# Gate and up stage of a quantised feed-forward: tokens of block n+2 quantised at the front of VectorE's block n, and GpSimd multiplying tiles 1, 3 and 5 instead of 2 and 4

## The reference, cut to what matters

```
def _act_fake_quant(x, clip_factor):
    scale = jax.nn.sigmoid(clip_factor) * jnp.max(jnp.abs(x)) / QMAX
    return jnp.clip(_ste_round(x / scale), -QMAX - 1.0, QMAX) * scale

xq = _act_fake_quant(x, clip_x[0])
gate = jnp.einsum('bsh,ih->bsi', xq, _weight_fake_quant(w_gate))
up = jnp.einsum('bsh,ih->bsi', xq, _weight_fake_quant(w_up))
h = _act_fake_quant(jax.nn.silu(gate) * up, clip_down[0])
return jnp.einsum('bsi,hi->bsh', h, _weight_fake_quant(w_down))
```

## Time and profile before

| what | us |
|---|---|
| median of 3 runs | 1045.89 (1040.85 to 1046.31) |
| the profiled execution, whole | 1039.43 |
| its span, first to last instruction | 1037.5 |
| start of the gate and up stage (first L1087) | 907.02 |
| its last GpSimd product ends | 982.90 |
| its last VectorE reduction (L1159) ends | 985.73 |
| `partition_all_reduce` starts | 988.85 |

### The profile page before, as it was taken

The page is one execution under the profiler, slowest core; times in us unless marked ns, Lnnn a source line. Parts: engine busy times, 40 slices in busy tenths (PEclk is TensorE's granted clock), DMA queues, the critical chain, the costliest instruction groups (busy, mean ns, idle before and its releaser), DMA issues. The chain is left out here.

```text
span 1037.5 us, 21991 instructions
## 1 busy us (share of the span) xinstructions
PE 797.6 (77%) x8184; PEld 443.3 (43%) x8184; DVE 903.3 (87%) x1428; ACT 644.2 (62%) x981; POOL 518.6 (50%) x330
## 2 busy tenths in 40 slices
PE   2789874777777679998888988988889869167656
PEld 1455541111111245555555555555556548022223
DVE  6679844999999889999989999999999987868968
ACT  3354563999999766555655655655656512467674
POOL 4132330000000019988888998888889877022300
PEclk9898896999999899999999999999999989689979
DMA  9489896564555565585555855577455446000013
GB/s 280 162 280 343 265 346 225 190 213 164 180 217 214 193 178 144 144 269 169 148 163 181 274 139 168 154 215 226 137 171 157 135 164 203 0 1 1 0 41 122
DMA packets 112400, 180.98 MB, mean 174 GB/s; under 512 B 10032, under 2 KB 37296, under 8 KB 112304
## 3 DMA queue, kind: packets, MB, share of 16 engines
q1 hardware_dynamic: 112304, 179.67, 54.5%
HBM read 137.70 MB, written 41.94 MB: 173 GB/s over the span
## 5 line engine op out<-in xcount | busy, mean ns | idle before, releaser
L786 POOL TENSOR_TENSOR e<-e,recip 128x768 f32<-128x768 f32 (+3 forms) x256 | 424.1, 1702 | 72.8 <-DVE recip L830 72.8
L763 ACT ACTIVATE e<-ps_att 128x512 f32<-128x512 f32 x512 | 278.9, 595 | 186.5 <-PE ps_att L698 186.5
L694 PE MATMUL ps_att<-shift,minus 128*128 128x512 bf16 x512 | 200.8, 392 | 21.0 <-DMA arena<-k_stack 8.7
L716 PE MATMUL acc<-e,arena 128*32 128x128 f32 x4096 | 170.1, 284 | 50.5 <-DVE e L798 36.5
L698 PE MATMUL ps_att<-arena 128*128 128x128 bf16 x2048 | 202.3, 222 | 0.0
L812 DVE TENSOR_TENSOR total<-total,e 128x512 f32<-128x512 f32 x240 | 168.0, 700 | 27.7 <-ACT e L763 3.3
L553 ACT ACTIVATE copies<-ps_max 128x1024 bf16<-128x1024 f32 x192 | 178.9, 1037 | 20.2 <-PE ps_max L533 20.2
L698 PEld LDWEIGHTS ps_att<-arena 128*128 128x128 bf16 x2048 | 160.7, 100 | 63.4 <-issue 5.1
L533 PE MATMUL ps_max<-q_head,k_head 128*128 128x512 bf16 x512 | 139.3, 387 | 59.1 <-DVE high L572 20.0
L821 DVE TENSOR_TENSOR total<-total,e 128x512 f32<-128x512 f32 x256 | 177.5, 693 | 2.0 <-ACT e L763 0.2
L716 PEld LDWEIGHTS acc<-e,arena 128*32 128x32 f32 x4096 | 105.0, 111 | 88.4 <-issue 54.0
(11 more groups left out here) (129 smaller groups left out, 858.0 us busy)
## 6 DMA issues: line engine op xcount, KB each, us to landing
arena<-k_stack SPq DMA_DIRECT2D x256, 256.0 KB, 2.8
k_stack<-parts SPq DMA_DIRECT2D x64, 256.0 KB, 3.9
q_stack<-parts SPq DMA_DIRECT2D x64, 256.0 KB, 3.7
k_head<-k_stack SPq DMA_DIRECT2D x16, 1024.0 KB, 5.6
q_head<-q_stack SPq DMA_DIRECT2D x16, 1024.0 KB, 7.8
arena<-q_stack SPq DMA_DIRECT2D x64, 256.0 KB, 4.4
arena<-in_x_dram SPq DMA_DIRECT2D x5, 1024.0 KB, 7.9
arena<-in_ctx_dram SPq DMA_DIRECT2D x4, 1024.0 KB, 6.6
```

The source lines that it names most:

```text
L694: nc.tensor.matmul(ps[half][:], minus[:], shift_at(qc, kc).to_broadcast([P, HB, P]), start=True, stop=False, skip_group_check=True)
L716: last = nc.tensor.matmul(acc[grp:grp + 32, col:col + P], vpad[:, kc, b, v_col:v_col + 32], e[:, slot(i), b * P:(b + 1) * P], start=False, ...
L763: nc.scalar.activation(e[:, slot(i), half * BANK:(half + 1) * BANK], ps[half][:], ACT.Exp, scale=DK ** -0.5).then_inc(exped, 1)
L786: nc.gpsimd.tensor_tensor(part, part, recip[:, kc % 2, :].rearrange("p (a q) -> p a q", a=1) .to_broadcast([P, share, P]), ALU.mult).then_ ...
```

## The change

`POOL_J` becomes (1, 3, 5), and with it `DVE_J` becomes (0, 2, 4). Waits that count products follow from these by `counts(k)`. In VectorE's queue `integers(n + 2)` moves from tile 4's place to tile 0's.

```
-        POOL_J = (2, 4)
+        POOL_J = (1, 3, 5)
...
-                            if j == 4 and n + 2 < NB:
+                            if j == 0 and n + 2 < NB:
                                 integers(n + 2)
```

## The result

Over 20 executions each the changed kernel takes 1036.91 us (median) and the kernel before 1043.50. The ratio is 0.994, with a 95% interval of 0.992 to 0.996: 6.6 us faster by the medians. The interval leaves out no change, though the gain is hardly more than the 5.2 us that I had called the least that can be told. I had forecast 0.9959 and 1041.6 us against a median of 1045.89.

What follows compares the result with a forecast made beforehand. A circle of waits through VectorE's conversion was taken as the bound. Blocks gain 5.81 us, the last block loses 1.55, net about -4.3: 1035.1 us profiled, 1041.6 on the median; own range 1039.6 to 1043.4, wider 1035.0 to 1047.0.

Steps and rivals of the forecast that it cites:

- What bounds the kernel now: Stage from 907 to 985 us: no engine full, a circle of waits between engines sets 8.95 us a block.
- The circle through the conversion: Conversion waits behind product 3, its silu behind transposes, those behind the conversion before; 8.95 us a block, 8.20 without rounding.
- my signs: Signs of being right: blocks 8.0 to 8.1 and 7.1 us, L1128 at 0.43, VectorE idle before each product until its silu.
- The walk of the new block: From silu 4 to the next block's silu 4: 8.05 us for 8.95, or 7.10 for 8.20 without the rounding.
- The third copy and the tiles: Moved tiles in blocks 1 to 6: ScalarE copy costs 0.57 us a block, already walked; VectorE loses a 0.66 product.
- Added waits cost nothing: Maxima on tiles 1, 3 and 5 wait for GpSimd multiplies; covered by product 2 and the conversion, so 0.
- L1128 and the multiplies pass each other: Second conversion runs between GpSimd multiplies at 0.43 us; a meeting makes it 1.37, price 0 to 0.1 a block, taken as 0.
- The stage's end: The all-reduce follows GpSimd's last multiply after a 5.95 us load, not VectorE's reduction, so it moves by -4.26 us.
- Rival 1: The stage ends with VectorE's last reduction instead: -5.6 us, so 1033.8, or 1040.2 on the median; chance 0.14.
- Rivals 2 and 3: Stage blocks: another circle closes near 8.8 us, 1046.5, chance 0.14; or VectorE bounds at 10.25 us, 1054.7, chance 0.07.
- The clock behind the idle stretch: Down stage's first matmuls after about 1 us longer idling: TensorE's clock costs between -1.8 and +1.8 us, taken as 0.
- From the profiled execution to the median: Ratio 0.9959 from the profiled 1039.43 us, carried to the three runs' median of 1045.89, gives 1041.6 us.

Runs made afterwards that it cites:

- the three banks: The changed kernel with its PSUM banks dealt as three gate and three up instead of two and four; ratio to the kernel before 0.990.
- conversion only: The kernel before with only the conversion moved to the front of VectorE's block, GpSimd keeping tiles 2 and 4; profiled 1032.31 us, ratio 0.990.
- its wait filled: The kernel before with 20 more TensorE transposes made before the conversion is awaited; ratio 0.9994 (0.9979 to 1.0009).
- warm start: 28 unused matmuls before the down stage, added to conversion at front, only tile 0 on GpSimd in the last block, 3 + 3 banks; 1024.92 us, ratio 0.982.

## Why the prediction came out as it did

- **What bounds the kernel now.** Right. The circle through the conversion is what the moved line cuts; alone it takes a block from 8.95 to 7.47. Of my signs one came in part: VectorE idles 0.56 and 0.77 us before the products of tiles 2 and 4, but not before product 0, where a maximum ends just as the silu does.
- **The walk of the new block.** Right to 0.01 us. From silu 4: gate matmul 0.86 (0.85 forecast), transposes 1.72 (1.72), tile 1 2.17 (2.17), silu 1 3.23 (3.24), silu 4 again 8.04 (8.05). Without rounding 7.10 (7.10). That two gate banks and ScalarE close it is shown by the three banks.
- **The third copy and the tiles.** I put its cost into the walk as 0.57 and did not say what the tiles cost by themselves. With the conversion at the front it is 8.04 - 7.47 = 0.57 a block, and 5.2 us at the all-reduce (77.71 - 72.53), some 4.5 when the quick block 0 of "conversion only" is taken off. The two halves of the change pull against each other. Alone they are +10.8 and -9.3, or some +6.8 and -8.6 without the three low-clock blocks of the one and the quick block 0 of the other; together they are -4.1.
- **Added waits cost nothing.** Right but for the last block, where a maximum waits 0.90 for GpSimd; that lies on the way to VectorE's end, which does not decide. L1128 and the multiplies pass each other, as taken. The trace agrees with the Trainium skill ("SBUF — State Buffer", section "SBUF: two separate sides") in both directions: 1.37 where they meet, 0.43 where they don't.
- **The stage's end.** Right, and the all-reduce follows GpSimd: -4.21 at the last multiply, for -4.26, and -4.12 at the all-reduce. Rival 1 falls: VectorE's L1159 moved by 5.50, and the all-reduce did not follow it. The Trainium skill ("GPSIMD Engine Reference", section "Instruction dispatch") gives 5.95 us for such a load. The trace has 5.95 and 6.04, and in the other kernels in which it showed 5.74 to 6.25.
- **Rivals 2 and 3.** No block from 1 to 6 near 8.8 or over it in any profiled execution with the conversion at the front; the longest took 8.05.
- **The clock behind the idle stretch.** I took 0 within 1.8 either way. The first 24 matmuls took 6.00 and 5.86 in the changed kernel, for 5.33, 5.35 and 5.61 before, so 0.3 to 0.7 us more. That the longer idle stretch makes this is not shown: the kernel before with its wait filled took 6.11, behind an idle stretch of 14.6 us, and the changed kernel's was 15.7. The whole way from L1222 is 49.32 and 49.20 in the changed kernel, for 48.67, 49.36 and 48.94 before, and these overlap. A term of 0 within 1.8 holds.
- **From the profiled execution to the median.** Here the forecast is thin. By the medians the gain is 6.6 us, a little outside the forecast's own -6.3 to -2.5, and 0.9959 lies at the upper end of the measured interval. The walk explains 4.1 us. The other 2.5 us are not one kernel's luck: in all seven measurements with the conversion at the front and no warm start the difference of the medians is larger than that of the all-reduce, by 2.5 to 4.4 us. With the wait filled, and the conversion at its old place, it is larger by 0.5 only. One candidate is the clock's fall in the old wait, in one of three executions of the kernel before (+5.1 us) and in none of the eight with the conversion at the front. But the filled wait ought then to have brought 1 to 2 us on the median, and did not show it. The spread of the kernels' times could hide that much, and no run shows another cause. So the 2.5 us stay open. That the ratio came out near the forecast rests on the stage, and for these 2.5 us on the width of the range. Single executions cannot settle it: the stage's first rounding, ahead of which all kernels are the same, came anywhere from 903.9 to 912.2 us.

## What to carry to other kernels

An instruction whose result is wanted a block later belongs at the front of an in-order queue, before anything that waits for the present block; find such circles by walking one period through all engines, by start-to-start distances. Test two edits made together apart, since here one was worth some 9 us and the other ate half of it. And when an engine changes its kind of instruction at a stage's end, its last ordinary instruction may set the end, not the semaphore that it waits for.

## What the runs showed of the hardware that I had not expected

- TensorE's clock can fall inside a stage where the engine is mostly busy: in one execution of the kernel before, after 5 us with TensorE busy 3.70 and a wait of 1.31, the granted clock was 0.66 over the next 5 us. It fell so in four blocks in a row: the first three took 1.1 to 1.25 us over 8.95, the last 1.7 over 8.20. The other two profiled executions of the same program had no such block.
- The instant at which the clock rises at a stage's beginning moves too. Block 0 of this stage was up to 0.8 us shorter in four of the thirteen profiled executions (silu 1 at 10.41 to 10.73, for 11.1 to 11.2), by nothing that the kernels do.
- The load behind GpSimd's last multiply runs while the engine waits for its semaphore. With 8.55 us between the last multiply's end (971.87 + 1.26) and the all-reduce (981.68) nothing of it is left.
- With the same block 0 and an even clock, the stage from first rounding to all-reduce repeats to 0.03 us (81.83 and 81.82, 77.71 and 77.68), while whole executions of one program spread over 8 to 14 us. For a change of one stage, that distance is the sharper measure, once the clock at its beginning has been compared.
